# Attention and a binary convolution on one core: a wider start, halved copies of the next x, statistics in three groups, convolution weights after the last scan

## The reference, cut to what matters

```python
# x: (4, 256, 64, 64), so N = 4096 positions and C = 256 channels per batch
f = einsum('kc,bcn->bkn', w1, xf) + b1            # 16 features per position
attention = softmax(einsum('bkn,bkm->bnm', f, f)) # 4096 x 4096 per batch
out = einsum('bcm,bnm->bcn', xf, attention)
x = x + out * 0.1
# then a 3x3 convolution with sign(x), sign(w) * alpha, batch norm (gamma, beta), plus x
```

## Time and profile before

| | us |
|---|---|
| median of 3 runs | 2083.57 (2081.54 to 2087.14) |
| the profiled execution: its own time | 2082.55 |
| its span, first to last instruction | 2080.8 |
| first exponential of tile 0 | 103.37 |
| last attend of tile 31 / first convolution product | 1851.67 / 1860.11 |

### The profile page before, as it was taken

One profiled execution on the slowest core, in us unless ns is written; L12 is line 12 of the kernel. 1 busy time (PEld: TensorE's weight loads), 2 busy tenths in 40 slices (PEclk: granted clock), 3 DMA queues, 4 the chain that ended last, 5 costly groups with the idle time before them and its releaser, 6 DMA issues. The chain is left out here.

```text
span 2080.8 us, 40199 instructions
## 1 busy us (share of the span) xinstructions
PE 1940.4 (93%) x15232; PEld 1636.3 (79%) x15232; DVE 1590.0 (76%) x2167; ACT 1435.3 (69%) x2829; POOL 1196.1 (57%) x791
## 2 busy tenths in 40 slices
PE   4499999999999999999999999999999999989990
PEld 1179998999789888997899999987899997854440
DVE  2477777888887888888787788888887787647778
ACT  2467777777777777777777777777777778643326
POOL 0265555666765555567755556667666664167760
PEclk6589999999999999999999999999999999999995
DMA  3311111012211111012111110021111003224019
GB/s 101 103 38 49 58 59 38 30 30 69 91 47 57 58 38 38 31 60 71 49 53 54 58 38 30 31 81 61 31 30 31 30 29 119 107 98 165 0 40 363
DMA packets 58278, 133.55 MB, mean 64 GB/s; under 512 B 9328, under 2 KB 9328, under 8 KB 57584
## 3 DMA queue, kind: packets, MB, share of 16 engines
q1 hardware_dynamic: 58096, 131.10, 18.7%
HBM read 84.48 MB, written 33.62 MB: 57 GB/s over the span
## 5 line engine op out<-in xcount | busy, mean ns | idle before, releaser
L670 POOL CAST Ph<-P 128x1024 fp32r<-128x1024 f32 x480 | 689.6, 1438 | 585.5 <-ACT P L461 585.0
L471 ACT ACTIVATE sc<-sc,nb 128x512 f32<-128x512 f32 x1024 | 676.2, 660 | 412.8 <-DVE nb L546 412.4
L546 DVE TENSOR_REDUCE nb<-sc 128x1 f32<-128x512 f32 x1024 | 695.2, 684 | 318.0 <-PE sc L381 317.7
L389 PE MATMUL acct<-Ph,xh 64*128 64x512 f32 x2048 | 811.8, 396 | 0.0
L389 PE MATMUL accb<-Ph,xh 64*128 64x512 f32 x2048 | 809.1, 395 | 1.5 <-ACT tb L481 1.3
L389 PE MATMUL accb<-Ph,xl 64*128 64x512 f32 x2048 | 803.5, 392 | 0.0
L389 PE MATMUL acct<-Ph,xl 64*128 64x512 f32 x2048 | 798.0, 390 | 0.0
L556 DVE TENSOR_TENSOR Pl<-P,Ph 128x1024 fp32r<-128x1024 f32 x512 | 664.2, 1297 | 53.8 <-POOL Ph L670 27.1
L389 PE MATMUL acct<-Pl,xh 64*128 64x512 f32 x2048 | 637.6, 391 | 0.0
L389 PE MATMUL accb<-Pl,xh 64*128 64x512 f32 x2048 | 635.0, 389 | 1.5 <-DVE Pl L556 1.4
L461 ACT ACTIVATE P<-ee 128x1024 f32<-128x1024 f32 x512 | 525.5, 1026 | 61.9 <-PE ee L373 42.8
(11 more groups left out here) (105 smaller groups left out, 1370.1 us busy)
## 6 DMA issues: line engine op xcount, KB each, us to landing
wk<-xt SPq DMA_DIRECT2D x32, 512.0 KB, 4.1
xres<-x SPq DMA_DIRECT2D x32, 512.0 KB, 4.3
x<-xres SPq DMA_DIRECT2D x32, 512.0 KB, 2.8
R<-rd SPq DMA_DIRECT2D x32, 256.0 KB, 3.2
xn<-x SPq DMA_DIRECT2D x16, 512.0 KB, 11.9
xr<-x SPq DMA_DIRECT2D x16, 512.0 KB, 11.2
out<-xr SPq DMA_DIRECT2D x16, 512.0 KB, 4.0
An<-x SPq DMA_DIRECT2D x14, 512.0 KB, 5.8
```

The costliest lines, as they stand in the source:

```text
L389: return pe.matmul(to[:], w[rows, g * GM + k, c * 128:(c + 1) * 128], p[rows, s, k * QC:(k + 1) * QC], start=g == 0 and i == 0, stop=g == ...
L471: nc.scalar.activation(sc[v % 2][:], sc[v % 2][:], ACT.Exp, bias=nb[:, t % 2, w:w + 1], accum_out=bsum[:, t % 2, w:w + 1]).then_inc(bsum_d ...
L546: nc.vector.tensor_reduce(nb[:, t % 2, w:w + 1], sc[v % 2][:], AX.X, ALU.max, negate=True).then_inc(nmax_done, 1)
L670: nc.gpsimd.tensor_copy(Ph[:, e % RP, :], P[:, e % 2, :]).then_inc(ph_done, 1)
```

## The change

- The head: for the first 22 steps one wide unit of 1024 scores takes the place of two blocks. Three PSUM buffers serve it (the scan's, the energies', the bottom sums'), one reduction and one exponential work on all 1024 columns. The first three projections come at once, the fourth at u = 4; the splits of the features move with them. A T row block is waited for in two semaphores, `ts_in` (the copy for scans) and `te_in` (the copy for energies). ACT runs a one-column exponential first of all. All eight x chunks of batch 0 are split before the first `round_p`. SP's order in the head changes.
- The next batch's x: a step now takes half a chunk; two of three steps have one. ACT copies it in step g, POOL subtracts in step g + 1. POOL's six operations move to steps 1, 3, 6, 9, 12, 15 (in tiles with q = 0: 2, 5, 8, 11, 13, 15). The store of a tile's result and the load of the next x move on SP from g = 14, 15 to g = 1, 2 of the next tile.
- Statistics: `row_max` at g = 7, the exponential at g = 8, `row_weights` at g = 9, `row_sum` at g = 10.
- The end: PA = 16 * 31; signs of the weights at g = 8, 10 of tile 30, sums at g = 9 to 14, absolute sums at g = 0, 1 of tile 31; x2 of batch 0 loaded at g = 3 of tile 31 (before: g = 15 of tile 30); image signs at g = 8, 9, 11, 12, transforms at g = 10, 13.

```diff
+        accb = ps("accb", [128, CT * QC])
+        scw = ps("scw", [128, GW])
+        wide = [scw, ee, accb]
-        PA = G * (NT - 2)
+        PA = G * (NT - 1)
+        UH = LAG - 2
+        HEAD_F = {0: (0, 1, 2), 4: (3,)}
+        HEAD_HL = {0: (0, 1), 2: (2,), 4: (3,)}
...
         def split_at(t, g):
-            if n % 3 or not 0 <= n // 3 < XG or not 0 < nxt < NB:
+            if n % 3 == 2 or not 0 <= n // 3 < XG or not 0 < nxt < NB:
-            return nxt * XG + n // 3
+            return 2 * (nxt * XG + n // 3) + n % 3
...  SP
+            for s in range(XP, SL):
+                load_piece(s)
             scan_rows(0)
             f_rows(0)
-            for s in range(XP, SL):
-                load_piece(s)
             scan_rows(1)
             for s in range(1, FU):
                 f_rows(s)
-            for m in range(XB):
-                load_xt(m)
+                load_xt(s - 1)
...
-                    if g == 14 and t >= 1:
-                        store_x2(t - 1)
-                    if g == 15 and 0 <= t < NT - 1:
-                        load_res(t + 1)
+                    if g == 1 and t >= 2:
+                        store_x2(t - 2)
+                    if g == 2 and t >= 1:
+                        load_res(t)
...  PE
+            def scan_wide(u):
+                t, j, i = unit_at(2 * u)
+                if u >= 3:
+                    pe.wait_ge(bsum_done, u - 2)
+                for k in range(2):
+                    mm = pe.matmul(wide[u % 3][:, k * 512:(k + 1) * 512], ...)
+                mm.then_inc(s_done, 1)
...  ACT
-                nc.scalar.copy(xh[:, k * 4:(k + 1) * 4, :], landed[m % XB]).then_inc(xh_done, 1)
+                nc.scalar.copy(xh[:, 2 * k:2 * k + 2, :], landed[m % XB][:, 2 * p:2 * p + 2, :]).then_inc(xh_done, 1)
-                if t == NT - 2 and g in (0, 2):
+                if t == NT - 2 and g in (8, 10):
...
-                if t == NT - 1 and g in (4, 6, 8, 10):
+                if t == NT - 1 and g in (8, 9, 11, 12):
...  POOL
-            for m in range(4):
-                lower_x(m)
+            for h in range(2 * XG):
+                lower_x(h)
...
-                if 0 <= e < 4:
-                    lower_x(4 + e)
+                part = None
                 if t >= 1:
-                    if g in (1, 4):
-                        scale_bottom(t - 1, g // 4)
...
+                    part = {k: i for i, k in enumerate((2, 5, 8, 11, 13, 15) if t % CH == 0 else (1, 3, 6, 9, 12, 15))}.get(g)
+                if part in (0, 1):
+                    scale_bottom(t - 1, part)
+                if part in (2, 4):
+                    join(t - 1, part // 4)
+                if part in (3, 5):
+                    add_x(t - 1, part // 5)
+                h = split_at(*divmod(n - 1, G))
+                if h is not None:
+                    lower_x(h)
...
-                if t == NT - 1 and g in (8, 12):
+                if t == NT - 1 and g in (10, 13):
```

More of the change, by code:

```diff
@@ L153, in attention @@
         hl_done = sem("hl_done")
-        t_in = [sem(f"t_in{k}") for k in range(2)]
+        ts_in = [sem(f"ts_in{k}") for k in range(2)]
+        te_in = [sem(f"te_in{k}") for k in range(2)]
         us_in = [sem(f"us_in{k}") for k in range(2)]
@@ L187, in attention, with unit_count, unit_at @@
         inner_done = sem("inner_done")
-        PA = G * (NT - 2)
+        PA = G * (NT - 1)
+        UH = LAG - 2
+        def unit_count(v):
+            return v + 1 - UH if v >= 2 * UH else v // 2 + 1
+        def unit_at(v):
+            t, w = divmod(v, SU)
+            pair, half = divmod(w, 2)
+            j, i = divmod(pair, QT)
+            return t, 2 * j + half, i
+        HEAD_F = {0: (0, 1, 2), 4: (3,)}
+        HEAD_HL = {0: (0, 1), 2: (2,), 4: (3,)}
         steps = [divmod(n, G) for n in range(-LAG, NG)]
@@ L238, in f_rows @@
                 sp.wait_ge(hl_done, s + 1)
-                for base in (S0, 0):
+                for base, landed_in in ((S0, ts_in), (0, te_in)):
                     for j in range(2):
@@ L352, in _ @@
                         load_x2(sp, x2d, 0, xn, r0_in)
+            store_x2(NT - 2)
             store_x2(NT - 1)
@@ L388, in attend @@
                 to = (acc_t, acc_b)[half][c]
-                return pe.matmul(to[:], w[rows, g * GM + k, c * 128:(c + 1) * 128], p[rows, s, k * QC:(k + 1) * QC],
+                return pe.matmul(to[:, :], w[rows, g * GM + k, c * 128:(c + 1) * 128], p[rows, s, k * QC:(k + 1) * QC],
                                  start=g == 0 and i == 0, stop=g == G - 1 and i == 5)
@@ L396, in _ @@
                 b = t // CH
[L397 to L400, removed]
+                for s in HEAD_F.get(u, ()):
+                    if s >= 2:
+                        pe.wait_ge(fp_done, s - 1)
+                    project(s, acc_t[s % 2])
                 if 0 <= e < NG:
@@ L403, in _ @@
                         pe.wait_ge(p_done, e)
+                    else:
+                        pe.wait_ge(bsum_done, (UH - 2) // 3 * 3 + 2)
+                    if e % (G * CH) == 0:
+                        for k in range(2):
+                            pe.wait_ge(te_in[k], 32 * (e // (G * CH) + 1) * FU // 2)
                     if held[0]:
@@ L447, in _ @@
                                 top.then_inc(av_done, 1)
-                    if c == 0 and u < NG:
+                    if c == 0 and UH <= u < NG:
                         scan(2 * u + 1)
@@ L466, in exps, with block_sum @@
                     nc.scalar.activation(Ph[:, e % RP, :], ee[:], ACT.Exp).then_inc(p_done, 1)
[L468 to L471, removed]
+            def block_sum(v, to):
+                t, j, i = unit_at(v)
+                w = j * QT + i
+                act.wait_ge(nmax_done, unit_count(v))
+                nc.scalar.activation(to, to, ACT.Exp, bias=nb[:, t % 2, w:w + 1],
                                      accum_out=bsum[:, t % 2, w:w + 1]).then_inc(bsum_done, 1)
@@ L488, in copy_f @@
                                      bias=col[0:S0 + KS, 0:1]).then_inc(fp_done, 1)
+            act.wait_ge(fill_done, 1)
+            nc.scalar.activation(dd[:, 0:1], sr[:, 31:32], ACT.Exp)
             act.wait_ge(col_in, 16)
@@ L493, in _ @@
                 e, u = n + 2, n + LAG
-                if u < G and u % 4 == 0:
-                    copy_f(u // 4, acc_t[u // 4 % 2])
+                for s in HEAD_F.get(u, ()):
+                    copy_f(s, acc_t[s % 2])
                 if g == 0 and t >= 1:
@@ L499, in _ @@
                     exps(e)
-                if u < NG:
-                    block_sum(2 * u)
+                if u < UH:
+                    block_sum(2 * u, wide[u % 3][:])
+                elif u < NG:
+                    block_sum(2 * u, sc[0])
                 if g == G - 1 and t >= 0:
                     copy_bottom(t, 0)
-                if u < NG:
-                    block_sum(2 * u + 1)
-                if g == 9 and 0 <= t + 1 < NT:
+                if UH <= u < NG:
+                    block_sum(2 * u + 1, sc[1])
+                if g == 8 and 0 <= t + 1 < NT:
                     act.wait_ge(dd_done, t + 2)
@@ L625, in _ @@
                 e, u = n + 2, n + LAG
-                if u < G and u % 4 == 0:
-                    split_f(u // 4)
+                for s in HEAD_HL.get(u, ()):
+                    split_f(s)
                 if g == 0 and t >= 1:
                     scale_top(t - 1, 1)
-                if u < NG:
-                    block_max(2 * u)
+                if u < UH:
+                    block_max(2 * u, wide[u % 3][:])
+                elif u < NG:
+                    block_max(2 * u, sc[0])
                 if 0 <= e - 1 < NG:
```

114 lines of the change are left out of this document (64 added, 50 removed).

## The result

| | before | after |
|---|---|---|
| median of the runs, us | 2082.56 (2081.38 to 2087.14) | 2013.68 (2013.15 to 2014.28) |
| ratio, 95% interval | | 0.9665 [0.9649, 0.9682] |
| span of the profiled execution | 2080.8 | 2011.8 |
| first exponential / first attend | 103.37 / 108.32 | 55.80 / 60.75 |
| tile 1 begins | 161.9 | 108.9 |

The forecast was 2015.0. The span's 69.0 divides as follows (a tile is counted from its first exponential to the next tile's): start to tile 1, -53.1; the six tiles q = 7 and q = 0, 321.6 against 341.5, -19.9; the other 23 tiles up to 29, +5.9; tile 30, -6.9; the gap, +4.5; tile 31 and convolution, +0.4 together.

What follows compares the result with a forecast made beforehand. PE was taken to set the step of 3.27 us in ordinary tiles, with losses at head, batch changes and tile 30. Terms -54.8 - 22 + 8.7 - 6.4 + 6.2 = -68.3 gave a median of 2015, range 1997 to 2035 (8 in 10).

Steps and rivals of the forecast that it cites:

- Head: Start to tile 1: wide units of 1.25 and early projections bring tile 1 to 107.0, -54.8 us.
- the lower one throughout: Head: three projections of 3.6 each end by 17.4, if PE's clock is the lower one throughout.
- it took 7.4: Head: from transposition to first exponential 7.4, as before, so the first exponential comes at 57.4.
- the two chains meet; `round_p` ends at 59.5, and the first attend follows: Head: P and POOL's x chunks are both ready at 58.4; `round_p` takes 1.04, then comes the first attend.
- Next batch's x: Three pairs of tiles at batch changes: halves instead of whole chunks, 53.2 a tile, -22 us (bounds -27 and 0).
- The rival by which halves meet Pl: Batch-change tiles: each of 48 halves delays Pl by 1.08, losing 0.27 each, 13 us in all: 2028; 14%.
- The edge: Tile edges: ACT's copy waits for POOL's last add_x, PE late by 0.3 at 29 edges, +8.7 us.
- The rival of no cost: Tile edges: PE's products for c = 1 can wait 0.3 in a gap, total 2006; 20%.
- that of a whole missed step: Tile edges: ACT behind POOL's add costs PE a whole step, 95 in place of 8.7: 2101; 3%.
- Tile 30: One ACT exponential instead of two while scans run, weights' signs after the scans: 59.0 to 52.6, -6.4 us.
- The gap: Between attention and convolution: later transforms, the second some 10.8, start the convolution later by 6.2 us.
- PE covers them: Ordinary tiles: the new places of the statistics' groups cost nothing.

Runs made afterwards that it cites:

- experiment 2: Changed kernel with the statistics back at their old steps (row_max g = 8, exponential g = 9, the rest g = 10): 2001.44 us, 0.9614 of the kernel before.
- experiment 9: Changed kernel with twelve of batch 0's sixteen x halves split before the first round_p, four in the first four steps: 2012.47 us, 0.9659 of the kernel before.
- experiment 10: Changed kernel with the second image transform moved from POOL's tile 31 to the start of POOL's convolution: 2008.64 us, 0.9643 of the kernel before.

## Why the prediction came out right

- **Head: -54.8 forecast, -53.1 measured.** The units came out at the forecast size: unit 4's maximum began at 28.09 (29.0 forecast), unit 15's ended at 43.01 (44.0), 1.24 a unit with 1.25 forecast. The reason given, that three buffers leave DVE and ACT no one to wait for, is wrong: DVE and ACT alone could go at 1.13, but a unit's scan takes PE 1.22 at the granted clock of 0.50 (34 to 42), and every third scan waits for its buffer. So the right size is partly luck.

  The second projection took 1.94, not 3.6, which the prediction had tied to "the lower one throughout". The granted clock was 1.00 there, the upper level of 2.4 GHz; the fourth projection, the same eight matmuls at 22.48, took 3.68 at 0.50, the lower level. (The clock reads 0.70 from 19.8 to 21.0: it fell there, and PE had been idle from 15.3 to 18.1.) The scan waited for T's DMAs all the same.

  The transposition ended at 50.28 (50.0 forecast). `wd` ahead of it took 1.25 at 46.73, 0.07 behind the start of a half on POOL, where it had taken 0.18 before: the collision of experiment 2, in the head.

  From there two steps failed. First, "it took 7.4" was carried over, and it took 5.5: before, SP still had three other DMAs to issue and sent the transposed rows 1.0 late (95.98 to 97.01), and the first energies were 0.8 longer because a scan between them waited for its buffer (100.90 to 102.51, now 54.14 to 54.95). So the first exponential came at 55.80, not 57.4. Second, "the two chains meet; `round_p` ends at 59.5, and the first attend follows": POOL did end at about the time forecast (59.3 against 58.4; a half is 0.62 + 1.27, a chunk 3.8 with 3.7 forecast), but nothing waited for it (experiment 9). The first attend came 4.95 behind the first exponential, not 2.1; that distance stood in the earlier trace rows and I did not use it. The errors, -1.6 and +2.9, left 1.25, and tile 0 took 0.6 more than forecast.
- **Next batch's x: -22 forecast, -19.9 measured**; 53.2 a tile was the forecast, 53.6 is the mean, 53.1 to 54.2. These six tiles hold six of the 29 edges, whose 1.8 the forecast has in the next term. The rival by which halves meet Pl (+13) had the meeting right for 36 of 48 halves and the price wrong: there Pl takes 0.2 to 0.8 longer, mostly 0.35 to 0.55, which is within the 0.81 that DVE has idle in a step, and not 1.08. The forecast's reason, that a half ends just before Pl begins, holds for twelve at most.
- **The edge: +0.3 at each, +8.7 forecast.** PE's step grew by 0.32 in the table's tile and the 23 tiles outside the six by 5.9, 0.26 each; moving the add gave 8.8 back. The rival of no cost and that of a whole missed step are both refuted.
- **Tile 30: -6.4 forecast, -6.9 measured. The gap: +6.2 forecast, +4.5 measured**, because the second transform took 8.8, not 10.8 (experiment 10). Why it was shorter stays open.
- **Statistics: "PE covers them" is wrong.** Against the kernel before, the price is nothing, as forecast; but only because the same collision was there before and moved along. It costs about 12 in the changed kernel (experiment 2), and the kernel before has the same step of 3.60. PE waiting within ordinary steps was the prediction's own sign of being wrong; it was there in both kernels, so the difference did not show it. I had taken an ordinary tile's full PE as proof that nothing waited. PE busy all the time and PE at its pace are not the same: waits of 0.3 don't show in the busy time.
- **The sum.** It lies within 1.3 of the measured median, closer than its terms: the head brought 1.7 less than forecast and the gap cost 1.7 less, and the two cancel by luck.

## What to carry to other kernels

Look at the pace of the bounding engine step by step, not at its busy time: a step of 3.6 among steps of 3.24 is a wait. When small DVE instructions and long POOL operations share a list of steps, place them in different steps, whatever the size of the DVE ones. And before a chain is taken to decide, measure the distance from its rival's event to the result in the kernel at hand: a distance that stays the same to 0.01 us while the rival's event moves shows that the rival does not decide.

## What was unexpected on the hardware

- A DVE subtraction of 128x4 took 0.15 alone and 1.25 behind a POOL operation of 1.30.
- The eight matmuls of a projection took 3.68 in a stretch with a granted clock of 0.50 and 1.94 in one with 1.00.
- A maximum over 128x1024 in PSUM took 1.22 (1.13 from one to the next) where two over 512 took 1.36; an exponential over 1024 with its sum took 1.09 + 0.19, 1.13 from one to the next.
